# Attention and recurrence on one core: a third dense bank until the first step, the mask's load apart from its scaling, and values as one 512-column product per batch

## The reference, cut to what matters

```python
# layer 1: causal attention of 16 heads of 32, with one more key and value that comes from cond
q, k, v = split(x @ c_attn_w + c_attn_b)
k = concat([cond @ uk_w.T + uk_b, k]); v = concat([cond @ uv_w.T + uv_b, v])
scores = where(kj <= qi + 1, q @ k.T / sqrt(32), -10000) + mask
x = x + (softmax(scores) @ v) @ c_proj_w + c_proj_b
# layer 2: a recurrence over the 512 positions, from h = cond
xw = x @ Wx + b
h_t = tanh(h_{t-1} @ Wh + xw_t)
x = x + h
```

## Time and profile before

| | us |
|---|---|
| median of 3 runs | 1801.43 (1799.96 to 1805.03) |
| the profiled execution | 1800.27 |
| its span in the trace | 1798.5 |
| PE busy | 1634.6 (91% of the span) |
| DVE busy | 888.8 (49%) |
| ACT busy | 709.9 (39%) |
| POOL busy | 149.6 (8%) |

### The profile page before, as it was taken

One profiled execution on the slowest core, in us unless ns is written; L12 is line 12 of the kernel. 1 busy time (PEld: TensorE's weight loads), 2 busy tenths in 40 slices (PEclk: granted clock), 3 DMA queues, 4 the chain that ended last, 5 costly groups with the idle time before them and its releaser, 6 DMA issues.

```text
span 1798.5 us, 67877 instructions
## 1 busy us (share of the span) xinstructions
PE 1634.6 (91%) x29292; PEld 1378.1 (77%) x29292; DVE 888.8 (49%) x2986; ACT 709.9 (39%) x2205; POOL 149.6 (8%) x248
## 2 busy tenths in 40 slices
PE   5788889898999998999999999898998998999997
PEld 4777778786878787877878788686886887887876
DVE  4444435454545455555555565465655574222222
ACT  2444545444344444444444444444444453111111
POOL 0110100010000100010111100011001000000000
PEclk8988989999999999999999999998998999999999
DMA  7744536443435464554545566554565561100000
GB/s 253 188 146 138 145 118 186 131 129 108 127 111 155 109 160 119 141 150 126 138 128 154 131 160 159 137 151 132 139 157 136 153 152 38 27 16 17 26 16 21
DMA packets 228442, 221.67 MB, mean 123 GB/s; under 512 B 22952, under 2 KB 187048, under 8 KB 227632
## 3 DMA queue, kind: packets, MB, share of 16 engines
q1 hardware_dynamic: 211568, 175.86, 37.0%
q0 software_dynamic: 16576, 41.46, 8.1%
HBM read 141.45 MB, written 75.76 MB: 121 GB/s over the span
## 4 chain that ended last, share of the span: by engine, by line
PE 72%; DVE 9%; DMA 7%; issue 5%; ACT 4%; SPq 2%; POOL 1%; DVEq 0%; POOLq 0%; ACTq 0%
PE rec L926 24%; PE turned L849 8%; PE dense L381 7%; PE dense L382 6%; PE dense L383 6%; PE pv L862 4%; PE scores L841 4%; PE scores L926 3%; PE dense L897 3%; DVE pre L753 3%; ACT hist L594 3%; DMA msk<-mask 2%; DMA x_dram<-x1nat 2%; PE pv L880 2%; DVE probs L688 1%
## 5 line engine op out<-in xcount | busy, mean ns | idle before, releaser
L926 PE MATMUL rec<-wh,hist 128*8 128x128 f32 x14336 | 483.7, 275 | 62.9 <-ACT hist L594 56.6
L926 PEld LDWEIGHTS rec<-wh,hist 128*8 128x8 f32 x14336 | 355.2, 94 | 145.5 <-ACT hist L594 103.9
L552 ACT ACTIVATE probs<-probs,nmax 128x128 f32<-128x128 f32 (+3 forms) x512 | 287.9, 563 | 220.6 <-DVE nmax L688 211.7
L594 ACT ACTIVATE hist<-pre 128x32 f32<-128x32 f32 x512 | 131.9, 258 | 576.7 <-DVE pre L763 340.4
L688 DVE CUSTOM_DVE_ANT_0 probs<-scores,msk,nimg 128x128 f32<-128x128 f32 (+3 forms) x512 | 276.2, 544 | 58.4 <-PE scores L841 56.5
L753 DVE STREAM_TRANSPOSE pre<-rec 128x128 f32<-128x128 f32 x448 | 141.3, 315 | 319.8 <-PE rec L926 317.4
L849 PE MATMUL turned<-ident,probs 128*128 128x128 f32 x1280 | 241.0, 288 | 1.9 <-DVE probsT L697 0.9
L841 PE MATMUL scores<-kq 96*128 96x128 f32 (+3 forms) x512 | 203.8, 403 | 37.7 <-DVE nmax L688 23.7
L849 PEld LDWEIGHTS turned<-ident,probs 128*128 128x128 f32 x1280 | 145.3, 141 | 65.3 <-issue 55.2
L697 DVE COPY probsT<-turned 128x128 f32<-128x128 f32 (+3 forms) x256 | 124.7, 487 | 97.0 <-PE turned L849 95.8
L559 ACT COPY probsT<-turned 128x128 f32<-128x128 f32 (+3 forms) x256 | 108.1, 422 | 147.9 <-PE turned L849 146.7
(11 more groups left out here) (119 smaller groups left out, 2293.1 us busy)
## 6 DMA issues: line engine op xcount, KB each, us to landing
kq<-kq_dram SPq DMA_DIRECT2D x96, 320.0 KB, 5.6
kq<-kq_dram SPq DMA_DIRECT2D x96, 256.0 KB, 4.7
kq<-kq_dram SPq DMA_DIRECT2D x96, 192.0 KB, 3.7
kq_dram<-qs_hi SPq DMA_DIRECT2D x128, 128.0 KB, 2.5
kq_dram<-ks_hi SPq DMA_DIRECT2D x128, 128.0 KB, 2.4
kq<-kq_dram SPq DMA_DIRECT2D x96, 128.0 KB, 2.6
xin<-x SPq DMA_DIRECT2D x32, 256.0 KB, 3.2
kq_dram<-qs_lo SPq DMA_DIRECT2D x64, 128.0 KB, 2.4
```

The lines of the kernel that those rows point to most:

```text
L552: act.activation(probs[:, g % PROBS, 0:n], probs[:, g % PROBS, 0:n], ACT.Exp, scale=-1.0, bias=nmax[:, e, h:h + 1], accum_out=rowsum[:, e, ...
L594: act.activation(hist[:, g // HALF % 2, :, :, g % HALF], pre[:, :, 0:B], ACT.Tanh).then_inc(h_ready, 1)
L926: last = pe.matmul(d[Q * j:Q * j + B, 0:P], hist[:, before // HALF, f, :, before % HALF], wh[:, f, P * j:P * j + P], start=f == 0 and not ...
```

## The change

Three edits. First, `rec` takes part in the rotation of the dense banks until the first step: `JOB` now holds a bank and how often it was used before, the modulus is 3 until then and 2 after it, and the first step waits for the last copy out of `rec`. Second, `mskload` in POOL's order keeps only the DMA, with a lag of 0.9 instead of 0.0; the wait for it, the scaling and the causal add are an event of their own, `mskscale`, which the main order emits in the tenth head of the 16 before those that use it (at the start: behind both loads), with a lag of 1.0. Third, a value item computes all 512 columns of one sequence in one bank, with 12 matmuls of 512 columns and a cost of 2.7, and DVE adds the bias to 128x512 at once.

```diff
-    "POOL": {"mskload": 0.0, "keep": 0.2, "vstore": 1.0, "x1n": 0.8, "finished": 0.0, "out": 1.0},
+    "POOL": {"mskload": 0.9, "mskscale": 1.0, "keep": 0.2, "vstore": 1.0, "x1n": 0.8, "finished": 0.0, "out": 1.0},
...
     def values(g, e):
-        return [("v", g, 2 * e, 1.5), ("v", g, 2 * e + 1, 1.5), ("vstore", g, e, 0.0)]
+        return [("v", g, e, 2.7), ("vstore", g, e, 0.0)]
...
-    emit([("xload", 0, 0, 0.0), ("xload", 1, 0, 0.0), ("mskload", 0, 0, 0.0), ("mskload", 0, 1, 0.0),
+    emit([("xload", 0, 0, 0.0), ("xload", 1, 0, 0.0), ("mskload", 0, 0, 0.0), ("mskload", 0, 1, 0.0), ("mskscale", 0, 0, 0.0), ("mskscale", 0, 1, 0.0),
           ("vimgload", 0, 0, 0.0), ("vimgload", 0, 1, 0.0)] + begin(0) + chunk(0, 0) + chunk(0, 1) + chunk(0, 2))
...
         if h2 == 9 and 0 < block <= 2 * TRIPS:
             emit([("attnlow", block - 1, 0, 0.0)])
+            if block + 1 < 2 * TRIPS:
+                emit([("mskscale", (block + 1) // 2, (block + 1) % 2, 0.0)])
...
-    JOB = {}
+    JOB, DONE, uses, turn = {}, {}, [0, 0, 0], 0
     for kind, g, i in ORDER["PE"]:
         if kind in DENSE_KINDS:
-            JOB[kind, g, i] = len(JOB)
+            n = turn % (2 if ("step", 0, 0) in JOB else 3)
+            JOB[kind, g, i] = n, uses[n]
+            uses[n] += 1
+            turn += 1
+            DONE[kind, g, i] = turn
+        elif (kind, g) == ("step", 0):
+            JOB[kind, g, i] = 2, uses[2]
...
+        banks = dense + [rec]
...
         def wait_bank(eng, kind, g, i):
-            n = JOB[kind, g, i]
-            if n > 1:
-                eng.wait_ge(dense_copied[n % 2], n // 2)
+            n, before = JOB[kind, g, i]
+            if before:
+                eng.wait_ge(dense_copied[n], before)
...
                     pool.dma_start(msk[:, i, 0:P * (p + 1)], mask[2 * r + i, 0, 0:1, 0:P * (p + 1)]
                                    .broadcast_to([P, P * (p + 1)])).then_inc(msk_loaded[i], 16)
+                elif kind == "mskscale":
                     pool.wait_ge(msk_loaded[i], 16 * (g + 1))
...
                 elif kind == "v":
                     wait_dense(dve, kind, g, i)
-                    e, half = divmod(i, 2)
-                    if half == 0:
+                    if g == 0:
                         dve.wait_ge(bv_loaded, 16)
-                        if g:
-                            dve.wait_ge(v_stored[e], 16 * g)
-                    cols = slice(half * D // 2, (half + 1) * D // 2)
-                    dve.tensor_tensor(vnew[:, e, cols], bank(kind, g, i)[:, 0:D // 2], bv[:, cols], ALU.add
+                    else:
+                        dve.wait_ge(v_stored[i], 16 * g)
+                    dve.tensor_tensor(vnew[:, i, :], bank(kind, g, i)[:, :], bv[:], ALU.add
...
                 elif kind == "v":
-                    e, half = divmod(i, 2)
-                    w0 = 2 * D + half * D // 2
+                    mine = slice(P * i, P * i + P)
                     for f in range(C):
-                        last = split_product(d[:, 0:D // 2], xT_hi[:, f, P * e:P * e + P], xT_lo[:, f, P * e:P * e + P],
-                                             wqkv_hi[:, f, w0:w0 + D // 2], wqkv_lo[:, f, w0:w0 + D // 2],
+                        last = split_product(d[:, :], xT_hi[:, f, mine], xT_lo[:, f, mine],
+                                             wqkv_hi[:, f, 2 * D:3 * D], wqkv_lo[:, f, 2 * D:3 * D],
                                              f == 0, f == C - 1)
...
                     elif g == 0:
                         pe.wait_ge(weights_loaded, WEIGHT_LOADS)
+                        wait_bank(pe, "step", 0, 0)
```

More of the change, by code:

```diff
@@ L319, in attention_recurrence @@
         dense_ready = sem("dense_ready")
-        dense_copied = [sem(f"dense_copied{i}") for i in range(2)]
+        dense_copied = [sem(f"dense_copied{i}") for i in range(3)]
         scores_ready = sem("scores_ready")
@@ L351, in bank @@
         def bank(kind, g, i):
-            return dense[JOB[kind, g, i] % 2]
+            return banks[JOB[kind, g, i][0]]
         def copied(kind, g, i):
-            return dense_copied[JOB[kind, g, i] % 2]
+            return dense_copied[JOB[kind, g, i][0]]
         def wait_bank(eng, kind, g, i):
-            n = JOB[kind, g, i]
-            if n > 1:
-                eng.wait_ge(dense_copied[n % 2], n // 2)
+            n, before = JOB[kind, g, i]
+            if before:
+                eng.wait_ge(dense_copied[n], before)
         def wait_dense(eng, kind, g, i):
-            eng.wait_ge(dense_ready, JOB[kind, g, i] + 1)
+            eng.wait_ge(dense_ready, DONE[kind, g, i])
         def wait_copied(eng, kind, g, i):
-            n = JOB[kind, g, i]
-            eng.wait_ge(dense_copied[n % 2], n // 2 + 1)
+            n, before = JOB[kind, g, i]
+            eng.wait_ge(dense_copied[n], before + 1)
         def heads_tile(group):
@@ L494, in _ @@
                 elif kind == "vstore":
-                    for n in range(2):
-                        wait_copied(pool, "v", g, 2 * i + n)
+                    wait_copied(pool, "v", g, i)
                     pool.dma_start(v_dram[2 * r + i, P * p:P * p + P, :], vnew[:, i, :]).then_inc(v_stored[i], 16)
@@ L529, in _ @@
                     if g:
-                        wait_dense(act, "v", g - 1, 3)
+                        wait_dense(act, "v", g - 1, 1)
                     act.copy(xT_hi[:, 2 * i:2 * i + 2, :], xin[:, g % 2, 2 * i:2 * i + 2, :]).then_inc(xT_high, 1)
```

## The result

The changed kernel takes 1758.01 us in the median (1745.16 to 1763.18, 4 runs) against 1803.23 of the kernel before beside it: a ratio of 0.9742, 95% interval 0.9713 to 0.9770. Run again in a later set it gave 1752.09 (1748.16 to 1763.64, 6 runs), a ratio of 0.9714 (0.9686 to 0.9742). The forecast was 1750, in a range from 1716 to 1779. The profiled execution took 1745.16, its span is 1743.3.

A forecast was written before the change was run, and what follows sets the result against it. PE bounds the kernel, 72% of the chain, so its idle time and the clock lost afterwards count. 1800.3 - 34.6 - 20 - 6 + 7 = 1746.7, +2 for kq loads, +1.2 for the median: 1750, range 1716 to 1779.

The forecast's parts named there:

- (a): Whole kernel: the forecast itself, 1750 us, own range 1726 to 1766; chance 0.66.
- (c): Recurrence on PE: all 22 value items make adjacent step pairs and the clock falls at five, 1774 us; chance 0.08.
- (d): Value product on PE: a 512-column matmul takes no longer than a 256-column one, 0.117 us, giving 1710; chance 0.04.
- (e): GpSimd's mask scaling comes late, so a block's first score waits: slower, 1828 us with ten such waits; chance 0.04.
- (f): DVE finds another wait at the x1nat copy; only bank and values count: no change, 1801 us; chance 0.04.
- (b): GpSimd's second x1nat store lands behind the mask load in most cases, so less is saved: 1765 us; chance 0.14.
- The mask order: GpSimd's mask load between the x1nat stores, scaling later: saves 34.6 us of PE idle time and 20 of clock.
- kq next: PE's scores: with DVE no longer stopped, some kq loads lose their slack and come late, costing 2 us.
- The third bank: Dense products before the first step: PE's waits for qs_lo and ks_lo shrink, saving 6 us (0 to 9.5).
- The values: 512-column value product: streaming and entries save 6.5 us, adjacent steps and emptier heads cost more; together +7 (-7 to +18).
- The pairs: Longer value items make 11.7 pairs of adjacent recurrence steps, each second step waiting 0.97 us for the tanh: +11.
- A clock of 0.95 or more in the first stage: Sign of being right: PE's granted clock at 0.95 or more during attention of the first block of positions.

The follow-up runs named there:

- experiment 7: The changed kernel with the mask load moved behind both stores of x1nat in GpSimd's order: 1744.57 us, ratio 0.9671 to the kernel before.
- kernels 5: The changed kernel with the value product again as two 256-column items, mask edit and third bank kept: 1738.20 us, ratio 0.9629 to the kernel before.
- 11: The changed kernel with 256-column value items, recurrence steps paced evenly and the mask load behind both x1nat stores: 1719.22 us, ratio 0.9537 to the kernel before.

## Why the prediction was right, and which of its terms were not

**The median and the rivals.** Forecast (a) held: 1750 against 1752 and 1758, with the mask order as the bulk of the gain and by its mechanism. That the total came so near is in part luck. By the single edits the mask's part was 5 us too large (52.6 forecast, 47.6 measured), the bank's 11.5 too small and the values' 2.5 too dear; against that stand 10 to 15 us which the parts lose together and for which the sum had no term. (c) is out: it wanted a pair behind all 22 value items, and there are 13 more. (d) is out by the spacing of 0.232 us, (e) since no wait for the mask appears at a block's first score, (f) by 45 us. Of rival (b), experiment 7 shows that the mask load does delay the store behind it, but at a small price: DVE waits 4.9 us in all for the stores, not the 14 of that case.

**The mask order.** Right, and the bulk. Forecast: 34.6 + 20, less 2 for kq next. Measured alone: 47.6. The stalls of 37.6 us are gone; the wait for kq took back 7.3 (13.8 to 21.1), where the term said 2. That leaves some 17 for the clock, by difference, 20 forecast. The profile itself shows less: from 50 us to the tail the clock takes 36.9 us before (busy time times what is missing to 1.00, over windows of 4 us) and 28.7 with the mask order alone. That execution was 8 us slower than the median of its kernel; in the changed kernel at 1745 the clock takes 22.0. So there is a clock term, and its size is known only as 8 to 17 us.

**The third bank.** Right in kind, wrong in size: 6 forecast (0 to 9.5), 17.5 measured alone. The waits did go. What failed is "saved: the waits for qs_lo and ks_lo", which gave no term for the clock that comes back with them (some 7 us by the profile), though the step before had priced just that for the mask. Some 4 us more, busy time at full clock, stay unexplained.

**The values.** The sum of +7 was near +4.5 by luck: two terms were wrong and their errors cancel. Nor can its upper bound of +18 be worked out from what stands there: no stream gain, +11 and +5 make +16. The stream's gain of 5.4 us did not exist; the bound of 0.234 was the true value, and wx, whose instructions are fp32 and not f32r, was the wrong neighbour. The rule of 131 ns for 512 columns ("TensorE: Matmul & The Clock Gate", Back-to-back issue gap, of the Trainium skill) is not borne out here either. The pairs were right: 11.7 forecast, 13 more in the order and 13 more full waits in the trace (33 against 20). But the first stage, for which +3 was charged, gained 6.7. And in the changed kernel the values cost 14 to 20 us, not 7, while beside the mask order with two banks they cost nothing (1754.3 and 1753.2): they undo what the bank gives, and the prediction added the two terms as if they were apart.

**The signs named in advance.** DVE's wait for x_dram under 10 us: 4.9. Nmax under 6: 0.2. Waits for qs_lo and ks_lo under 3: 1.5. Spacing of 0.22: 0.232. Twelve more waits of 0.97: 13. A clock of 0.95 or more in the first stage: 0.93 (0.92 up to the first step), the one that failed; in that stage lies most of what the sum of the single gains (60.6 us) lacks (45 and 51 measured).

## What to carry to other kernels

Price a stall at its idle time plus what the clock loses after it, for small ones too: 9.5 us of bank waits were worth 17.5, some 7 of them clock. Where two edits relieve the same stage, price them together; each alone may give what both give. In an order written out by hand, a long item leaves fewer places for a chain of dependent steps: where it saved no engine time it cost 4.5 us alone, 14 to 20 beside mask and bank, and nothing beside the mask order alone. Spacing the steps evenly was worth 16 us, about as much as the bank.

## What the runs showed of the hardware

An f32r matmul of 512 columns in a stream of loads and matmuls starts every 0.232 us, one of 256 every 0.117: twice the columns take twice the time, so the weight load sets the pace of neither. What the clock does after a stall doesn't follow from the stall's length alone: in the same place a stall of 4.00 us was followed by a granted clock of 0.60, one of 2.65 by 1.00 and one of 2.27 by 0.57. One program spread over 1.1% (1745 to 1764 us, ten runs), its mean clock between 0.980 and 0.967, while kernels 5 and 11 spread over 0.3% and less (four and five runs).
